# Cosine attention, second layer: GpSimd's powers half batch by half batch, and three PSUM copies on VectorE instead of ScalarE

## The reference

```python
Q, K = l2norm(heads(x @ Wq.T)), l2norm(heads(x @ Wk.T));  V = heads(x @ Wv.T)   # 16 heads of 16
cos = clip(Q @ K.T, -0.999, 0.999)                       # 2048 x 2048 for each head and batch entry
W = maximum(1 - arccos(cos) / pi, 1e-6) ** 16
out = (W @ V) / (sum(W, -1) + 1e-6) @ Wo.T + bo
```

## Time and profile before

| | busy us | share of the span | instructions |
|---|---|---|---|
| PE matmuls | 4122.8 | 57% | 17232 |
| PE weight loads | 1407.8 | 20% | 17232 |
| DVE | 6747.7 | 94% | 5995 |
| ACT | 6510.5 | 91% | 3866 |
| POOL | 3153.3 | 44% | 1408 |

### The profile page before, as it was taken

The page is one execution under the profiler, slowest core; times in us unless marked ns, Lnnn a source line. Parts: engine busy times, 40 slices in busy tenths (PEclk is TensorE's granted clock), DMA queues, the critical chain, the costliest instruction groups (busy, mean ns, idle before and its releaser), DMA issues. The chain is left out here.

```text
span 7175.6 us, 55838 instructions
## 1 busy us (share of the span) xinstructions
PE 4122.8 (57%) x17232; PEld 1407.8 (20%) x17232; DVE 6747.7 (94%) x5995; ACT 6510.5 (91%) x3866; POOL 3153.3 (44%) x1408
## 2 busy tenths in 40 slices
PE   6767666666667667455454454454544554545445
PEld 3222222222222232111111121111111111211113
DVE  7899999999999947999999999999999999999995
ACT  3699999999999924999999999999999999999994
POOL 0244444444444400454554545545545445455452
PEclk8898889888888877555556566655665666656656
DMA  3100000000000033000000000000000000000002
GB/s 129 52 18 13 18 12 18 12 18 12 18 13 17 8 140 101 6 8 15 8 8 15 8 14 8 10 11 8 8 15 8 8 15 8 14 8 8 14 4 98
DMA packets 247526, 165.84 MB, mean 23 GB/s; under 512 B 149326, under 2 KB 231145, under 8 KB 245946
## 3 DMA queue, kind: packets, MB, share of 16 engines
q1 hardware_dynamic: 242746, 159.51, 7.7%
q10 hardware_dynamic: 4608, 4.20, 0.2%
HBM read 99.94 MB, written 63.70 MB: 23 GB/s over the span
## 5 line engine op out<-in xcount | busy, mean ns | idle before, releaser
L1029 PE MATMUL psS<-q_stack,k_stack 96*128 96x512 bf16 x2048 | 1014.6, 600 | 1675.9 <-DVE work L1178 1615.0
L1235 POOL TENSOR_TENSOR work<-work 128x1584 f32<-128x1584 f32 (+1 forms) x688 | 1908.4, 2810 | 6.9
L705 POOL TENSOR_SCALAR work<-work 128x2048 f32<-128x2048 f32 x512 | 970.5, 1896 | 1528.7 <-DVE work L912 1274.1
L1232 POOL TENSOR_SCALAR work<-work 128x1584 f32<-128x1584 f32 (+1 forms) x172 | 261.6, 1521 | 2387.0 <-ACT work L1148 2387.0
L1173 DVE TENSOR_SCALAR work<-psS 128x1024 f32<-128x1024 f32 x1024 | 1205.4, 1218 | 82.6 <-PE psS L1029 56.5
L900 DVE SCALAR_TENSOR_TENSOR work<-work,psS 128x1024 f32<-128x1024 f32 x1024 | 1212.3, 1210 | 51.2 <-ACT work L858 50.4
L1178 DVE TENSOR_TENSOR work<-psS,work 128x1024 f32<-128x1024 f32 x1024 | 1199.8, 1212 | 0.0
L858 ACT ACTIVATE work<-psS 128x1024 f32<-128x1024 f32 x1024 | 1064.1, 1039 | 120.0 <-PE psS L723 87.4
L1184 DVE SCALAR_TENSOR_TENSOR work<-work 128x2048 f32<-128x2048 f32 x512 | 1139.6, 2282 | 34.3 <-ACT work L1144 33.7
L723 PE MATMUL psS<-q_stack,k_stack 102*128 102x512 bf16 x2048 | 719.3, 438 | 712.1 <-DVE work L900 675.9
L873 ACT ACTIVATE work<-work 128x2048 f32<-128x2048 f32 x512 | 987.5, 1929 | 2.6 <-POOL work L705 2.2
(11 more groups left out here) (140 smaller groups left out, 3986.9 us busy)
## 6 DMA issues: line engine op xcount, KB each, us to landing
qk_parts<-work SPq DMA_DIRECT2D x64, 384.0 KB, 3.2
q_stack<-qk_parts SPq DMA_DIRECT2D x384, 64.0 KB, 2.3
k_stack<-qk_parts SPq DMA_DIRECT2D x384, 64.0 KB, 2.3
xT_store<-work SPq DMA_DIRECT2D x2, 4096.0 KB, 15.9
ffn_in<-xT_store SPq DMA_DIRECT2D x64, 128.0 KB, 2.5
work<-y_store SPq DMA_DIRECT2D x8, 1024.0 KB, 13.9
work<-in_x SPq DMA_DIRECT2D x1, 4096.0 KB, 14.1
xn_store<-work SPq DMA_DIRECT2D x1, 4096.0 KB, 13.1
```

The lines of the kernel that those rows point to most:

```text
L705: nc.gpsimd.tensor_scalar(slot, slot, F32_MAX, 0.0, ALU.min, ALU.max).then_inc(s_m, 1)
L1029: last = nc.tensor.matmul(m.psS[half][:, q * 512:(q + 1) * 512], m.k_stack[b][0:ROWS, kt * P:(kt + 1) * P], m.q_stack[b][0:ROWS, c:c + 512 ...
L1235: nc.gpsimd.tensor_tensor(parts[i % 2], parts[i % 2], parts[i % 2], ALU.mult).then_inc(s_pp, 1)
```

## The change

- The column split 0 / ACT_POW / DVE_POW / 2048 goes from 1328, 192, 528 (ScalarE, VectorE, GpSimd) to 1296, 160, 592.
- GpSimd does the affine step and the four squarings of half 0, then those of half 1, each instruction waiting for the one before. TensorE's wait on `s_pp` becomes 5 per half.
- The two Relus, the FFN result's copy and the head copy are issued by VectorE, between the units of its clip loop: the FFN copy after the first unit, the head copy after the second, the first Relu after the third, the second Relu after the last. They fall in the same batch as before, or the Relus one VectorE turn ahead, which is the same stretch of time.

```diff
-    ACT_POW, DVE_POW = 1328, 1520
+    ACT_POW, DVE_POW = 1296, 1456
...
-                pe.wait_ge(s_pp, 2 * STEPS * j + STEPS + 4 if chunk % 2 else STEPS * chunk)
+                pe.wait_ge(s_pp, STEPS * chunk)
...
         @block.scalar
         def _(act):
-            def out_copy(n): ...
-            def relu(n): ...
-            def ffn_out(n): ...
-            def ffn_part(i): ...
...
         @block.vector
+            def relu(n, k):
+                if k == 0 and n > 0:
+                    dve.wait_ge(s_yps, n)
+                g = 1 - k
+                dve.wait_ge(s_h, 2 * n + k + 1)
+                nc.vector.tensor_scalar(m.hidden[:, 4 * g:4 * g + 4, :],
+                                        m.psM[g][:, :].rearrange("p (f t) -> p f t", f=4), 0.0, None, ALU.max)\
+                    .then_inc(s_r, 1)
+            def ffn_out(n):
+                dve.wait_ge(s_yps, n + 1)
+                if n > 0:
+                    dve.wait_ge(s_yst, 16 * n)
+                nc.vector.tensor_copy(m.ffn_out[:, :], m.psM[0][:, 0:D]).then_inc(s_yo, 1)
+            def out_copy(n):
+                dve.wait_ge(s_pv, KT * (n + 1))
+                if n > 0:
+                    dve.wait_ge(s_ot, n)
+                nc.vector.tensor_copy(m.head_outT[:, :], m.psO[n % B][:, :]).then_inc(s_o, 1)
...
-                if i + 1 < NB:
-                    for g in range(starts[i + 1], starts[i + 2]):
-                        clip_and_square(g)
+                units = range(starts[i + 1], starts[i + 2]) if i + 1 < NB else []
+                tiles = [n for n in range(TILES) if last_batch[n - 1] + 2 == i]
+                for at in range(max(len(units), 4)):
+                    if at < len(units):
+                        clip_and_square(units[at])
+                    for n in range(TILES):
+                        if at == 0 and last_batch[n - 1] + 3 == i:
+                            ffn_out(n)
+                        if at == 1 and last_batch[n] + 1 == i:
+                            out_copy(n)
+                    for n in tiles:
+                        if at == 2:
+                            relu(n, 0)
+                        if at == max(len(units), 4) - 1:
+                            relu(n, 1)
...
         @block.gpsimd
             for j in range(NB):
-                parts = [cosine(j, p, size)[:, :, DVE_POW:T] for p, size in thirds(j)]
-                for c, part in enumerate(parts):
-                    pool.wait_ge(s_at, 2 * j + c + 1)
+                for c, (p, size) in enumerate(thirds(j)):
+                    part = cosine(j, p, size)[:, :, DVE_POW:T]
+                    chunk = 2 * j + c
+                    pool.wait_ge(s_at, chunk + 1)
                     nc.gpsimd.tensor_scalar(part, part, 2.0 / PI, 0.5, ALU.mult, ALU.add).then_inc(s_pp, 1)
-                for i in range(2, 2 * STEPS):
-                    pool.wait_ge(s_pp, 2 * STEPS * j + i - 1)
-                    nc.gpsimd.tensor_tensor(parts[i % 2], parts[i % 2], parts[i % 2], ALU.mult).then_inc(s_pp, 1)
+                    for i in range(1, STEPS):
+                        pool.wait_ge(s_pp, STEPS * chunk + i)
+                        nc.gpsimd.tensor_tensor(part, part, part, ALU.mult).then_inc(s_pp, 1)
```

More of the change, by code:

```diff
@@ L1105, in _ @@
         def _(act):
[L1106 to L1131, removed]
             for i in range(NB + 2):
@@ L1140, in _ @@
                             .then_inc(s_ls, size)
-                    ffn_part(i)
                     act.wait_ge(s_ls, starts[i + 1])
@@ L1157, in _ @@
                         nc.scalar.activation(part, part, ACT.Exp, scale=16.0).then_inc(s_w, 1)
[L1158 to L1162, removed]
         @block.vector
```

## The result

The changed kernel takes 7125.9 us (median of 5 runs, 7119.72 to 7129.04) against 7163.72 (5 runs): ratio 0.9946, 95% interval 0.9931 to 0.9960. It is 38 us faster. 76 were forecast (7086, range 7054 to 7122), so the time lies outside the range on the slow side. All times are us.

The account below looks back on a forecast made before the run. ScalarE was taken to bound ordinary batches. 88.7 removed from it, less 7.7 and 6 in tile batches, plus 2 from gaps, less 1 in the last batches, gave 76 saved: 7162.6 to 7086 us, range 7054 to 7122.

Parts of the forecast that it names:

- What bounds an ordinary batch: Batches without FFN and head output: ScalarE's own work plus a 0.24 gap sets the period, 48.68 falling to 47.98.
- hand-over cost: Delay between dependent GpSimd multiplies: taken as 0.03 each, from VectorE's row, putting GpSimd's end at +34.3.
- the bound of 0.14: Upper hand-over cost considered per dependent GpSimd instruction; GpSimd would end at +35.2, the run another 11 us slower.
- The limit of +35.0: Latest end of GpSimd's powers, counted from the batch's first arctangent, that still fits ScalarE's period of 47.98.
- end + 13.0: Period if GpSimd holds VectorE's first affine step: GpSimd's end plus 5.3 powers and 13.4 tangents, less 5.55.
- The slower rival: GpSimd becomes the bound: with 0.45 per hand-over it ends at +37.7, period 50.7, total 7260; chance 6%.
- VectorE's own balance: VectorE loses 0.97 per batch on powers (-82) and gains the copies and Relus (+68), 14 less overall.
- VectorE is the bound: Rival: ScalarE's relief is worthless, only VectorE's balance counts, 14 gained, 7149; chance 6%.
- Tile batches gain 1.08 + 0.32 less these, some 29 in all.: The 32 batches with FFN and head output gain removed Relus and narrower powers, less score waits and Relu delays.
- the mix of waits of before (10, 12, 9): Tile batches with no, one or two VectorE waits for scores: about 10 at 49.4, 12 at 50.1 to 50.3, 9 at 51.5.
- waits of L1173 for scores about 36 as now: Sign that the forecast holds: VectorE's number of waits for TensorE's scores stays near 36.
- more waits for scores: Rival: all 32 tile batches get both waits for scores, 28 more x 1.15 = 32, giving 7118; chance 10%.

Follow-up runs that it names:

- the alternating run: The changed kernel, but GpSimd alternates between the two halves as before the change, now with 592 columns: 7248.28 us, ratio 1.0116 to the kernel before.
- the copies alone: The kernel before with only the Relus and copies moved to VectorE, columns and GpSimd's order as before: 7172.09 us, ratio 1.0010.
- the same pair: Both bias matmuls of a tile issued at the start of TensorE's turn, in the changed kernel (7082.19 us) and in the kernel before (7137.03 us).
- biases first: The changed kernel with both bias matmuls of a tile at the start of TensorE's turn, where it is idle: 7082.19 us, ratio 0.9883 to the kernel before.

## Why the prediction was wrong

**What bounds an ordinary batch: right.** ScalarE's chain plus 0.24. Forecast 47.98, all alike; measured 48.10, alike in 52 of 53 batches. The gain there was 42 (average 48.90 to 48.11, by the profiles) against 48. The missing 0.12 (6 in all) is mostly the output copy: it was priced at 0.38, but the Ln in front of it overlapped it by 0.10, and the table load that now follows Ln doesn't overlap (3513.89 + 10.62 + 0.02 = 3524.53 above). Removing it gave 0.28. An instruction's price is its start-to-start gap with the same neighbour as after the edit.

**GpSimd: right, its hand-over cost missed.** +34.3 forecast, +34.65 measured. A multiply that needs its predecessor starts 0.08 behind its end ((12.83 - 3.15) / 3 = 3.23 apart), not 0.03 as on VectorE; the bound of 0.14 held it. The limit of +35.0 fits: at +34.65 the hold on VectorE cost nothing and 0.39 of waiting was left behind it, which puts the limit near +35.0 (an estimate); at +38.7, in the alternating run, the kernel was 122 slower than the change. No run lies between the two. (The rival's "end + 13.0" adds its own terms wrongly: 5.3 + 13.4 - 5.55 is 13.15.) The slower rival was one scheduling decision away.

**VectorE's own balance: right.** Relu 0.60 start to start (3621.16 to 3621.76), powers 5.3 without disturbance (3621.76 to 3627.09 by the timeline) as forecast. The rival "VectorE is the bound" is false for the whole change and true for the copies alone.

**Tile batches: the step that failed.** "Tile batches gain 1.08 + 0.32 less these, some 29 in all." Measured: 50.14 and 49.85 on average in two profiles of the kernel before, 50.05 and 50.03 in two of the changed one; nothing gained, 30 short. The sum held the mix of waits of before (10, 12, 9) as given, and the sign "waits of L1173 for scores about 36 as now" failed with 58. With the waits taken out of both kernels, tile batches went from 49.16 to 48.49, 21 in all; so about 22 of the 30 are the waits behind the bias groups, and by the medians of the same pair 18 (44 - 26). The prediction had this mechanism as its rival "more waits for scores", priced at 32 and given 10%; it came about for 22 to 25 of 32 tile batches rather than all. That these waits are the loss is shown by the pair; what makes the biases slow more often is not.

The other 8 (12 by the medians) are sizes. Two Relus were priced at 1.08, but the Ln in front overlaps them (5457.24 + 1.91 against 5459.06, rows 6) and not the table load that now follows it (3621.27 + 1.91 + 0.02 = 3623.20): from the last Ln to the table load it was 2.90 and is 1.93, so removing them gave 0.97, and a batch with two waits gained 0.94 (51.51 to 50.57). And where nothing waits for scores, the first Relu delays the square by its whole 0.60: with biases first, ScalarE's Ln waits for the square in every tile batch (20.3 in all, one wait of 4.4, so 0.5 in the others) where the prediction counted 0.3 for batches without a wait, and a tile batch gained about 0.7 (49.4 to 48.7) and not 1.08 + 0.32 - 0.3 = 1.1.

**Profile against median.** The offset of 14.8 between the profiled execution of before and the median was carried over. The changed kernel's profiled execution lay only 3 above its median, so the first two profiles show 48 gained and the medians 38; the second two (7169.89 and 7132.74) show 37. The second profile of the kernel before had 28 waits for scores instead of 36 and was 9.3 shorter from the first batch to the last, all of it in tile batches (50.14 to 49.85): the count of slow biases is part of what makes executions of this kernel differ.

## What to carry to other kernels

- When two engines are both full, moving work from one to the other pays only if the receiver is relieved first, in the same edit. Test both halves together.
- A count of waits in one profile need not be a property of the code: it was 36 and 28 in two executions of one kernel, and 58 and 56 after a change that touched no matmul. Where a wait hangs on whether an instruction falls in slow clock, price it in the sum for all of its occurrences, and better take it out of the way: moving two bias groups into idle time was worth more here (44) than the whole change (38).
- A second engine that shares work is to be judged by when it ends against the next step of its neighbour. Half batch by half batch it ended at +34.65 and cost nothing; alternating, with the same work, it ended at +38.7 and made the kernel slower.

## What the runs showed of the hardware

- A two-input multiply on GpSimd that waits for the one in front of it costs 0.08 more than its own time (3.23 start to start for 3.15), against 0.04 of overlap for independent neighbours (2.79 for 2.83); 32 columns more in each of three units cost 0.16 (2.83 at 1584 columns, 3.15 at 1776).
- VectorE's fp32 affine step, SBUF to SBUF, was held until GpSimd's running multiply had ended (one took 3.26 instead of 0.48 in the batch shown of the alternating run). The other way round, GpSimd's affine step took up to 2.70 instead of 1.67 in 73 of 168 cases of that run, and up to 2.17 instead of 1.51 in 84 of 168 with the copies alone, each time beside VectorE's tangent, which has two inputs in SBUF. Clips and squares with an operand in PSUM took 1.21 to 1.23 beside GpSimd's multiplies in all runs.
- TensorE stayed at a granted clock of 0.50 (1.2 GHz) in slices that the profile shows wholly filled (4.00 of 4.00, the fp32 hidden layer between the bf16 scores), and reached 1.00 (2.4 GHz) in other tile batches with the same instructions and less of the time filled (2.90 of 4.00).
